# Rotation, normalisation and key splits placed on other engines in a two-layer attention kernel, with new orders for every queue

## The chip, the cores and the metric

The kernel runs on one core of a Trainium2 chip. The metric is the device time of one execution in microseconds (us). The engines are TensorE (PE; PEld is its weight load), VectorE (DVE), ScalarE (ACT), GpSimd (POOL) and SyncE (SP), whose queue issues all transfers (DMA). Each engine works through its own queue in the order in which the program wrote it; semaphores tie the queues together.

## The reference

Two layers, each an attention block and a mixture-of-adapters block, on 2048 rows of 512 (8 sequences of 256, float32). The layers differ in the attention's weights only and, in the source, in how these are stored. Cut to what matters:

```python
def attention(x, w_qkv, w_o):                 # 32 query heads, 8 key/value heads of 16
    q, k, v = split(x @ w_qkv)
    q, k = rope(q), rope(k)                   # pairs (x1, x2) -> (x1 c - x2 s, x1 s + x2 c)
    p = softmax(where(causal, q @ k.T / 4, -inf))
    return (p @ v) @ w_o

def ffn(x):                                   # 8 experts, top 2, rank 16
    w, sel = top_k(x @ gate_w.T, 2); w = softmax(w)
    return x @ base_w.T + base_b + 2 * sum(w[e] * (x @ A[e].T) @ B[e].T)

for layer in (a, b):
    x = x + attention(layernorm(x), *weights[layer])
    x = x + ffn(layernorm(x))
```

## The kernel before

**Tiles.** A tile s is one sequence of 256 rows in one layer: 16 tiles, 0 to 7 layer a, 8 to 15 layer b. The weights lie in SBUF; those of the attention are replaced between tiles 7 and 8 (`wd` fetches them into `Wst`, `wh` rounds them, `split` takes the low half). Every float32 product is done as three products of rounded and remainder parts (high and low: XH/XL, WQh/WQl, R/Rh, OH/OL).

**One tile.** `stats` (VectorE) gives mean and variance, `power` (GpSimd) the reciprocal root rs, `norm` (VectorE, L1064) the normalised rows xn, twice per norm, c = "a" ahead of attention and "f" ahead of the ffn. `tr` transposes xn on TensorE, `high` (ScalarE) and `low` (VectorE) split it. `q01` and `q2` make queries, keys and values in a PSUM tile each; `qe` (ScalarE) copies them out, the queries into R, keys and values into KV. `sw` (DMA) fetches the rows swapped in pairs into Qs. The rotation is `rc` (times cosine), `rs_` (Qs times sine), `ra` (sum), each in three parts b: 0 and 1 are halves of the queries, 2 the keys. Then `rh`, `kh` (ScalarE) round and `rl`, `kl` take the remainders, and twelve stores `st(p, 0..2)` by DMA bring R, Rh and the keys into the layout QK of four pairs of head groups p = 4 s to 4 s + 3. For each p: `A` (scores for the maxima), `Am` (VectorE, L1077, three maxima into nm), `M2` (transposes nm), `mc`, `mr` (the maxima back into QK), `B` (scores with the maximum taken off), `ex` (ScalarE, L929, exponent into PT), `causal` (GpSimd, L1237, mask, for i = 0 and 2). Two p make a half h = 2 s, 2 s + 1: `PV` (L534), `oe`, then the sums go round: `lc` (DMA), `rp` (VectorE, reciprocal), `rd`, `rr` (DMA, through memory, into NR), `mu` (GpSimd, L238, product), `oh`, `ol`. `oM` is the output product and `ox` (L1110) the residual add from PSUM. The ffn is `fA`, `fE`, `fG` (top 2), `gate_exp`, `gr`, `gt`, `fH`, `fW`, `lora_high`, `lora_low`, `fB`, `fC`, and `fx` (L1150) the second residual add; `store` and `xl` move the rows of X.

**PSUM.** There are four tiles PP0 to PP3 of [128, 2, 512]. The last arguments of a TensorE step are the tile and the release that it waits for: `q2(6, 0, 0, 3, ("qe01", 7))` goes into PP3 once `qe` has emptied the queries of tile 6.

**Order.** Each engine's queue is a list written out at the end of its block: tile s + 1's norm, products and rotation are threaded between tile s's attention and ffn. A step whose wait isn't met holds all that stands behind it on its engine. `qe(s, 0)` waits for all twelve stores of tile s - 1, since it writes R, from which they read; these in turn wait until B of four p before has read QK.

In the start, SyncE's queue is a list of loads; `kr` and `qk` lay constant rows into QK (qk waits for kr's data), and tile 0's swaps `sw(0, 0)`, `sw(0, 2)` come behind them.

## Time and profile before

| | us |
|---|---|
| median of 3 runs | 820.34 |
| range of the runs | 818.52 to 826.51 |
| the profiled execution | 823.84 |
| its span, first to last instruction | 821.8 |
| TensorE busy in the span | 685.9 (83%) |
| VectorE | 557.8 (68%) |
| GpSimd | 473.8 (58%) |
| ScalarE | 372.7 (45%) |
| mean granted TensorE clock | 0.901 of 2.4 GHz |

The profiled execution is one execution, 0.4% above the median. Busy times leave out waits and the issue of transfers. The chain of waits follows the work that ended last back from the last instruction, at each step to what released it.

### The profile page before, as it was taken

The numbers are of one execution on the slowest core, as the hardware profiler recorded it, in microseconds if no ns is written. First come the engines' busy times: TensorE is split into PE (matmuls) and PEld (weight loads), VectorE is DVE, ScalarE is ACT, GpSimd is POOL, SyncE is SP. The second block draws the span as 40 slices with busy tenths as digits, with TensorE's granted clock in tenths as the row PEclk, the third lists the DMA queues.
The fourth block names the chain that finished last, engine by engine and source line by source line (L and its number), as shares of the span: only waits on it lengthen the run. The fifth ranks groups of instructions, "written<-read, shape, count | busy, mean of one in ns | idle before, by whom it ended". The sixth has DMA issues, their size and how long they took to land.

```text
span 821.8 us, 18302 instructions
## 1 busy us (share of the span) xinstructions
PE 685.9 (83%) x7498; PEld 513.9 (63%) x7498; DVE 557.8 (68%) x786; ACT 372.7 (45%) x554; POOL 473.8 (58%) x446
## 2 busy tenths in 40 slices
PE   5826788898988897897988899887988889888996
PEld 4715565775666666665667676665667766564574
DVE  4377484766768795876868697775869686467453
ACT  2324554644544453454536464543535453453521
POOL 1124384757657593755849385865858474673621
PEclk7955959898999999798999999998999998997899
DMA  9551726163453636255452625354452725444111
GB/s 335 111 150 48 158 65 139 60 145 115 95 152 73 161 88 166 83 126 162 92 161 63 167 86 137 127 101 139 91 163 54 175 68 114 110 96 109 41 52 52
DMA packets 49650, 95.14 MB, mean 116 GB/s; under 512 B 7936, under 2 KB 19840, under 8 KB 49568
## 3 DMA queue, kind: packets, MB, share of 16 engines
q1 hardware_dynamic: 49568, 93.98, 43.6%
q8 instruction: 59, 0.97, 0.5%
q14 instruction: 23, 0.19, 0.1%
HBM read 24.42 MB, written 10.49 MB: 42 GB/s over the span
## 4 chain that ended last, share of the span: by engine, by line
PE 44%; DVE 16%; issue 13%; DMA 8%; POOL 7%; ACT 6%; SPq 5%; DVEq 0%; POOLq 0%; ACTq 0%
PE PP L428 27%; PE PP L534 11%; DVE nm L1077 5%; ACT PT L929 4%; PE PP L520 3%; POOL PT L1237 3%; DVE R L231 3%; PE PP L441 2%; POOL NE L238 2%; DMA Qs<-R 2%; DVE XL L1038 1%; DVE tw L1134 1%; DVE xn L1064 1%; DMA QK<-Rh 1%; DMA QK<-R 1%
## 5 line engine op out<-in xcount | busy, mean ns | idle before, releaser
L1077 DVE TENSOR_REDUCE nm<-PP 128x4 f32<-128x1024 f32 (+1 forms) x192 | 228.6, 1215 | 74.8 <-PE PP L428 74.2
L1237 POOL TENSOR_SCALAR_AFFINE_SELECT PT<-PT 128x1024 f32<-128x1024 f32 x128 | 144.4, 1133 | 153.8 <-ACT PT L929 153.7
L929 ACT ACTIVATE PT<-PP 128x1024 f32<-128x1024 f32 x192 | 193.2, 1026 | 83.8 <-PE PP L520 83.0
L428 PE MATMUL PP<-QK 64*128 64x128 f32 (+1 forms) x1024 | 102.6, 310 | 39.7 <-DVE nm L1077 10.5
L534 PE MATMUL PP<-PT,V 128*32 128x512 f32 x768 | 110.8, 720 | 21.0 <-POOL PT L1237 19.2
L428 PEld LDWEIGHTS PP<-QK 64*128 64x128 f32 x1024 | 85.9, 212 | 55.0 <-issue 21.6
L428 PE MATMUL PP<-XH,WQh 64*128 64x256 f32 x768 | 95.7, 299 | 6.1 <-DVE XL L1038 5.0
L520 PE MATMUL PP<-QK 64*128 64x512 f32 x384 | 83.3, 444 | 9.4 <-ACT PT L929 3.0
L428 PE MATMUL PP<-XL,WQh 64*128 64x256 f32 x768 | 91.0, 287 | 0.0
L428 PE MATMUL PP<-XH,WQl 64*128 64x256 f32 x768 | 90.8, 286 | 0.0
L238 POOL TENSOR_TENSOR NE<-NE,NR 128x512 f32<-128x512 f32 x30 | 41.2, 1374 | 69.1 <-DMA NR<-sums 69.1
L1064 DVE TENSOR_SCALAR xn<-X,mv,rs 128x512 f32<-128x512 f32 x64 | 49.3, 776 | 45.8 <-POOL rs L1228 26.7
L428 PEld LDWEIGHTS PP<-XH,WQh 64*128 64x128 f32 x768 | 69.9, 194 | 11.6 <-issue 5.2
L534 PEld LDWEIGHTS PP<-PT,V 128*32 128x32 f32 x768 | 25.5, 126 | 81.8 <-issue 60.4
L861 ACT ACTIVATE NE<-PP 128x1024 f32<-128x1024 f32 x32 | 32.8, 1024 | 86.0 <-PE PP L534 86.0
L205 POOL TENSOR_TENSOR Qs<-Qs,trig 128x512 f32<-128x512 f32 (+1 forms) x47 | 52.8, 1135 | 31.8 <-DMA Qs<-R 25.7
L428 PEld LDWEIGHTS PP<-XL,WQh 64*128 64x128 f32 x768 | 67.4, 194 | 0.6
L428 PEld LDWEIGHTS PP<-XH,WQl 64*128 64x128 f32 x768 | 67.3, 194 | 0.0
L428 PE MATMUL PP<-WOh,OH 64*128 64x512 f32 x256 | 56.1, 430 | 1.7 <-ACT mT L861 0.8
L428 PE MATMUL PP<-WBh,XH 64*128 64x512 f32 x256 | 54.5, 416 | 2.5 <-DVE glo L1114 2.3
L428 PE MATMUL PP<-WOh,OL 64*128 64x512 f32 x256 | 53.5, 408 | 0.0
L428 PE MATMUL PP<-WOl,OH 64*128 64x512 f32 x256 | 53.5, 408 | 0.0
...
## 6 DMA issues: line engine op xcount, KB each, us to landing
QK<-Rh SPq DMA_DIRECT2D x64, 256.0 KB, 4.4
...
Qs<-R SPq DMA_DIRECT2D x32, 256.0 KB, 2.4
...
```

What stands on the lines that cost most here:

```text
L205: e.tensor_tensor(schunk(b), schunk(b), trigs(1, b), ALU.mult).then_inc(S[f"rs{b}"], 1)
L231: ins = e.tensor_tensor(key_blocks(KL, q), key_tile(q), key_blocks(KH, q).bitcast(F32), ALU.subtract)
L238: e.tensor_tensor(n, n, NR[:, :], ALU.mult).then_inc(S["mu"], 1)
L428: ins = e.matmul(t[:, k, c], lhs(rows, which[k]), rhs(rows, which[k]), start=start, stop=stop, skip_group_check=True)
L441: ins = e.transpose(t[:, k, c:c + 64], source[rows, :], iden[rows, 64 * k:64 * k + 64])
L520: ins = e.matmul(PP[t][:, a, :].rearrange("p (j q) -> p j q", j=4), keys(g, a, 4 if i == 2 else 0), x[:, :, min(i, 1), :], start=True, sto ...
L534: ins = e.matmul(PP[t][32 * c:32 * c + 32, min(i, 1), :], V[:, s % 2, i // 2, 4 * G + c, :], PT[:, (3 * p + i) % RING, 512 * a:512 * a + 5 ...
L861: return e.activation(dst, src, ACT.Copy)
L929: e.activation(PT[:, k % RING, :].rearrange("p (a x) -> p a x", a=2), PP[t][:, :, :], ACT.Exp, scale=0.25).then_inc(S["ex"], 1)
L1064: e.tensor_scalar(xn[:, f, :], X[:, 2 * (s % XR) + i, :], mv[:, f, i, 0:1], rs[:, f, i:i + 1], ALU.subtract, ALU.mult).then_inc(S[c + "xn" ...
L1077: e.tensor_reduce(o, x, AX.X, ALU.max).then_inc(S["m"], 1)
L1237: e.affine_select(out=blk, in_=blk, compare_op=ALU.is_ge, fill=0.0, base=0, pattern=[[0, 8], [1, 128]], channel_multiplier=-1).then_inc(S[ ...
```

## The change

- `norm` moves from VectorE to ScalarE, as one Identity with scale rs and bias nb = -mean x rs. For it `eps` (ScalarE, two instructions of two columns) takes the place of ve's add, and `power` on GpSimd gets a second product nb.
- `rc` is no longer done in SBUF (it was on GpSimd nearly always), but on VectorE straight from PSUM, one instruction for the 1024 queries' elements and one for the keys' 256; it waits for `qe`, and for the stores of the tile before. `qe` copies into a buffer of its own, Qf, and waits only for the swaps of the tile before. The PSUM tiles are released by `rc01` and `rc2` instead of `qe01` and `qe2`.
- The rotated keys live in two blocks of KL (K2); KV is gone.
- `ra` of the keys, `rl` of both halves and `kl` are done by GpSimd (tile 0's `rs_(0, 0)`, `rs_(0, 2)`, `ra(0, 0)`, `rl(0, 0)` are VectorE's).
- The gate's difference gd is folded into the exponent (bias and scale, two instructions); te has a place of its own.
- nm has 16 columns instead of 128, and mT one buffer instead of two, so that `mc(p)` waits for `mr(p - 1)`.
- Wst is 1024 columns instead of 1536: one slot for the 768-wide weights.
- The orders of all five queues are new.

```diff
-        wland += [Wst[:, c:c + 768] for c in (0, 768, 0, 768)]
-        wland += [Wst[:, c:c + 512] for c in (0, 512, 1024, 0)]
+        wland += [Wst[:, 0:768]] * 4
+        wland += [Wst[:, c:c + 512] for c in (0, 512, 0, 512)]
 ...
+        K2 = KL.rearrange("p (n t) -> p n t", t=128)[:, 2:5:2, :]
+
+        def roped(b):
+            return QR[:, 2 * b:2 * b + 2, :].bitcast(F32) if b < 2 else K2.bitcast(F32)
 
 ...
-        def rope_rc(e, w, s, b):
-            w.wait_ge(S["c_trig"], 16)
-            w.wait_ge(S["sw01" if b < 2 else "sw2"], 32 * (s + 1))
-            e.tensor_tensor(qchunk(b), qchunk(b), trigs(0, b), ALU.mult).then_inc(S[f"rc{b}"], 1)
 ...
-            for g in range(4):
-                w.wait_ge(S[f"st{g}"], 48 * s)
 ...
             def wd(k):
-                w.wait_ge(S["wlp"], {17: 13, 18: 13, 19: 14, 20: 15, 21: 16, 22: 17, 23: 17, 24: 18}[k])
+                w.wait_ge(S["wlp"], {17: 13, 18: 14, 19: 15, 20: 16, 21: 17, 22: 17, 23: 18, 24: 19}[k])
 ...
-                x = QR.bitcast(F32) if b < 2 else KV[:, 0:1, :]
-                e.dma_start(Qs[0:P:2, c, :], x[1:P:2, :, :]).then_inc(done, 16)
-                e.dma_start(Qs[1:P:2, c, :], x[0:P:2, :, :]).then_inc(done, 16)
+                e.dma_start(Qs[0:P:2, c, :], Qf[1:P:2, c, :]).then_inc(done, 16)
+                e.dma_start(Qs[1:P:2, c, :], Qf[0:P:2, c, :]).then_inc(done, 16)
 ...
-            rows0(0); load(3); rows0(1); const("id"); load(7); load(0); rows(1); load(13); load(2); const("trig")
-            load(1); load(15); load(6); load(4); load(10); load(8); load(12); load(16); rows(3); load(5); rows(4)
-            const("iota"); rows(2); load(14); load(9); load(11); kr(); const("bias"); qk(); sw(0, 0); sw(0, 2)
 ...
+            rows0(0); rows0(1); rows(1); const("id"); load(16); load(1); load(0); const("trig"); load(6); load(5)
+            kr(); load(14); load(3); load(13); load(4); load(7); load(2); load(10); load(15); rows(3); rows(4)
+            load(8); load(9); rows(2); load(11); const("iota"); load(12); const("bias"); qk(); sw(0, 0); sw(0, 2)
+            st(0, 0); st(1, 0); st(2, 0); st(3, 0); st(0, 1); st(1, 1); st(2, 1); st(0, 2); st(3, 1); st(1, 2)
+            st(2, 2); st(3, 2); sw(1, 0); sw(1, 2); wd(17); mr(0); mr(1); st(4, 0); st(4, 1); st(4, 2); mr(2)
 ...
-            q01(6, 3, 1, 3); M2(20, 1, ("m", 62)); A(21, 0, 0, ("ex", 60)); tr("f", 6, 2, ("m", 63))
-            PV(9, 1, ("mc", 21)); tr("f", 7, 2); B(20, 0, 0, ("m", 64)); q2(6, 0, 0, 3, ("qe01", 7)); q2(6, 1, 0, 3)
 ...
+            tr("f", 6, 0, ("m", 62)); q01(6, 2, 1, 2); M2(20, 1, ("m", 63)); q01(6, 3, 1, 2); A(21, 0, 3, ("ex", 60))
+            tr("f", 7, 0); PV(9, 1, ("mc", 21)); q2(6, 0, 0, 3, ("m", 64)); q2(6, 1, 0, 3); B(20, 0, 0, ("fl", 4))
+            q2(6, 2, 0, 3); B(20, 1, 1, ("oe", 10)); q2(6, 3, 0, 3); A(21, 1, 2, ("rc01", 7)); q2(6, 0, 1, 3)
 ...
                 if b < 2:
                     w.wait_ge(S["q01"], 8 * s + 8)
-                    for g in range(4):
-                        w.wait_ge(S[f"st{g}"], 48 * s)
-                    copy(R[:, 0:1024].bitcast(F32).rearrange("p (f x) -> p f x", f=2), PP[t][:, :, :]).then_inc(
-                        S["qe01"], 1)
+                    w.wait_ge(S["sw01"], 32 * s)
+                    copy(Qf[:, 0:4, :].rearrange("p (f c) t -> p f (c t)", f=2), PP[t][:, :, :]).then_inc(S["qe01"], 1)
                 else:
                     w.wait_ge(S["q2"], 8 * s + 8)
-                    w.wait_ge(S["kl"], s)
+                    w.wait_ge(S["sw2"], 32 * s)
                     w.wait_ge(S["vt"], s)
-                    copy(KV[:, :, :], PP[t][:, :, 0:256]).then_inc(S["qe2"], 1)
+                    copy(Qf[:, 4:6, :], PP[t][:, :, 0:256]).then_inc(S["qe2"], 1)
+
+
+            def eps(c, s):
+                f = int(c == "f")
+                w.wait_ge(S["ng" + c], 2 * s + 2)
+                w.wait_ge(S["np" + c], 2 * s)
+                e.activation(ve_[:, f, :], mv[:, f, :, 1], ACT.Copy, bias=EPS).then_inc(S["ne" + c], 1)
+                e.activation(nme[:, f, :], mv[:, f, :, 0], ACT.Copy, scale=-1.0).then_inc(S["ne" + c], 1)
+
+            def norm(c, n):
+                f, i, s = int(c == "f"), n % 2, n // 2
+                w.wait_ge(S["np" + c], 2 * s + 2)
+                w.wait_ge(S[c + "t"], n)
+                e.activation(xn[:, f, :], X[:, 2 * (s % XR) + i, :], ACT.Identity, bias=nb[:, f, i:i + 1],
 ...
-                w.wait_ge(S[f"md{p % 2}"], 16 * (p // 2))
-                copy(mT[:, p % 2, :].rearrange("r (f t) -> r f t", f=2), PP[t][0:16, :, 0:64]).then_inc(S["mc"], 1)
+                if p:
+                    w.wait_ge(S[f"md{(p - 1) % 2}"], 16 * ((p + 1) // 2))
+                copy(mT[:, :].rearrange("r (f t) -> r f t", f=2), PP[t][0:16, :, 0:64]).then_inc(S["mc"], 1)
 ...
-                w.wait_ge(S["ng" + c], 2 * s + 2)
-                w.wait_ge(S["np" + c], s)
-                e.tensor_scalar(ve_[:, f, :], mv[:, f, :, 1], EPS, None, ALU.add).then_inc(S["ne" + c], 1)
-
-            def norm(c, n):
-                f, i, s = int(c == "f"), n % 2, n // 2
-                w.wait_ge(S["np" + c], s + 1)
-                w.wait_ge(S[c + "t"], n)
-                e.tensor_scalar(xn[:, f, :], X[:, 2 * (s % XR) + i, :], mv[:, f, i, 0:1], rs[:, f, i:i + 1], ALU.subtract,
-                                ALU.mult).then_inc(S[c + "xn"], 1)
 ...
+            def rc(s, b, t):
+                w.wait_ge(S["c_trig"], 16)
+                w.wait_ge(S["qe01" if b < 2 else "qe2"], s + 1)
+                for g in range(4):
+                    w.wait_ge(S[f"st{g}"], 48 * s)
+                if b < 2:
+                    e.tensor_tensor(QR.bitcast(F32), PP[t][:, :, :].rearrange("p f (c x) -> p (f c) x", c=2),
+                                    trig[:, 0, :].unsqueeze(1).to_broadcast([P, 4, 256]), ALU.mult).then_inc(S["rc01"], 1)
+                else:
+                    e.tensor_tensor(roped(2), PP[t][:, 0, 0:256].rearrange("p (q x) -> p q x", q=2), trigs(0, 2),
+                                    ALU.mult).then_inc(S["rc2"], 1)
 ...
-            stats("a", 0); norm("a", 0); split(0); norm("a", 1); split(1); low("a", 0, 0); split(2); split(3)
-            stats("a", 1); norm("a", 2); norm("a", 3); low("a", 1, 3); split(4); rs_(0, 0); split(5); rc(0, 2)
-            split(6); split(7); rc(0, 0); split(12); ra(0, 0); split(13); split(14); ra(0, 2); rl(0, 0); split(15)
-            kl(0); split(16); split(8); split(9); split(10); split(11); stats("a", 2); Am(0, 0, 0); Am(0, 1, 2)
 ...
+            stats("a", 0); split(0); split(1); low("a", 0, 0); split(2); split(3); stats("a", 1); rc(0, 0, 1)
+            rc(0, 2, 2); low("a", 1, 3); rs_(0, 0); rs_(0, 2); ra(0, 0); split(4); split(5); rl(0, 0); split(6)
+            split(7); split(12); split(13); split(14); split(15); split(16); split(8); split(9); split(10); split(11)
 ...
+            Am(20, 2, 1); Am(21, 0, 3); stats("a", 7); low("f", 3, 0); rc(6, 0, 2); Am(21, 1, 2); Am(21, 2, 0); rp(9)
 ...
-                w.wait_ge(S["ne" + c], s + 1)
+                w.wait_ge(S["ne" + c], 2 * s + 2)
                 w.wait_ge(S[c + "xn"], 2 * s)
                 e.tensor_tensor(rs[:, f, :], ve_[:, f, :], half[:, :], ALU.pow).then_inc(S["np" + c], 1)
+                w.wait_ge(S["np" + c], 2 * s + 1)
+                e.tensor_tensor(nb[:, f, :], nme[:, f, :], rs[:, f, :], ALU.mult).then_inc(S["np" + c], 1)
 ...
-            causal(19, 0); power("f", 3); mu(8); causal(19, 2); ol(8); addbias(3); power("a", 7); causal(20, 0)
 ...
-            causal(23, 0); mu(10); power("f", 4); ol(10); causal(23, 2); power("a", 8); addbias(4); causal(24, 0)
 ...
+            causal(19, 0); power("f", 3); mu(8); causal(19, 2); addbias(3); ol(8); power("a", 7); rs_(6, 0)
+            causal(20, 0); ra(6, 0); rs_(6, 1); causal(20, 2); ra(6, 1); rs_(6, 2); ra(6, 2); rl(6, 0); causal(21, 0)
+            rl(6, 1); kl(6); causal(21, 2); gt(3); mu(9); fH(3); ol(9); causal(22, 0); causal(22, 2); causal(23, 0)
+            power("f", 4); mu(10); causal(23, 2); addbias(4); ol(10); power("a", 8); rs_(7, 1); causal(24, 0)
```

## Rows read from the trace of the kernel before

**Rows 1.** Three stretches: us, then busy us of PE, PEld, DVE, ACT, POOL, PEclk, DMA, GB/s.

```profile
0.00:120.00 120.00, 74.53 (x754) 60.09 (x756) 68.82 (x89) 45.30 (x67) 46.08 (x46) 0.71 0.52 146
120.00:740.00 620.00, 541.32 (x6126) 405.93 (x6125) 444.97 (x616) 300.10 (x443) 398.51 (x368) 0.94 0.46 117
740.00:821.80 81.80, 70.01 (x622) 47.85 (x620) 43.99 (x83) 27.28 (x44) 29.16 (x32) 0.88 0.21 62
sum 821.80, PE 685.86 PEld 513.87 DVE 557.77 ACT 372.69 POOL 473.75; mean PE 228.62 PEld 171.29 DVE 185.92 ACT 124.23 POOL 157.92
```

**Rows 2.** VectorE in order of time (start us, us, what): L1150 of tiles 0 and 12.

```profile
177.50 1.16 DVE L1150 TENSOR_TENSOR X<-PP,X 128x1024 f32<-128x1024 f32 x1
...
742.42 1.22 DVE L1150 TENSOR_TENSOR X<-PP,X 128x1024 f32<-128x1024 f32 x1
```

**Rows 3.** What TensorE waited for (us in total, times, longest us).

```profile
PE PP L534 <- POOL PT L1237: 19.2, 6, 4.1
PE PP L441 <- DVE xn L1064: 19.2, 7, 5.1
...
PE PP L428 <- DVE nm L1077: 10.8, 12, 1.9
```

**Rows 4.** Chain of waits around 420 us (start us, us, what).

```profile
419.08 3.69 issue
422.81 1.26 POOL NE L238
...
424.77 1.60 DVE xn L1064
```

**Rows 5.** The five us behind one stall, columns as in rows 1.

```profile
189.00:194.00 5.00, 5.00 (x24) 0.79 (x16) 3.11 (x5) 1.03 (x1) 3.99 (x3) 0.50 0.33 104
```

**Rows 6.** Chain of waits in the start.

```profile
26.62 10.53 DMA Qs<-R
...
45.64 1.06 ACT Rh L861
```

**Rows 7.** TensorE in order of time, its first long stands (idle before, releaser).

```profile
50.97 0.48 PE L441 MATMUL PP<-iden,KV 64*128 64x64 f32 x4 [13.10 <-ACT KV L861]
...
57.33 2.08 PE L428 MATMUL PP<-QK 64*128 64x128 f32 x16 [5.88 <-issue]
```

**Rows 8.** VectorE's groups: xcount | busy us, mean ns | idle before.

```profile
L1064 DVE TENSOR_SCALAR xn<-X,mv,rs 128x512 f32<-128x512 f32 x64 | 49.3, 776 | 45.8 <-POOL rs L1228 26.7 <-PE PP L441 19.1
...
L231 DVE TENSOR_TENSOR R<-KV,R 128x384 fp32r<-128x384 f32 (+1 forms) x32 | 33.6, 1088 | 0.8 <-ACT R L861 0.7
...
L1110 DVE TENSOR_TENSOR X<-PP,X 128x1024 f32<-128x1024 f32 x16 | 19.6, 1222 | 7.8 <-PE PP L428 7.7
...
L215 DVE TENSOR_TENSOR R<-R,Rh 128x512 fp32r<-128x512 f32 x16 | 18.2, 1138 | 3.7 <-ACT Rh L861 3.7
L210 DVE TENSOR_TENSOR KV<-KV,Qs 128x256 f32<-128x256 f32 x16 | 14.0, 876 | 0.9 <-POOL Qs L205 0.9
...
L1058 DVE TENSOR_SCALAR ve<-mv 128x2 f32<-128x2 f32 x32 | 11.8, 368 | 1.1
```

**Rows 9.** The tile xn: duration ns min/median/max.

```profile
L1064 DVE TENSOR_SCALAR xn<-X,mv,rs x64: 532/546/2099, 7.6 to 802.7; 128x512 f32<-128x512 f32 x64
```

**Rows 10.** Two of ScalarE's groups.

```profile
L861 ACT ACTIVATE OH<-NE 128x512 fp32r<-128x512 f32 x32 | 20.0, 624 | 72.6 <-POOL NE L238 69.6 <-DVE NE L238 3.0
...
L861 ACT ACTIVATE R<-PP 128x1024 f32<-128x1024 f32 x16 | 16.4, 1022 | 56.7 <-DMA QK<-Rh 26.8 <-DMA QK<-R 20.7 <-PE PP L428 9.1
```

**Rows 11.** Two of GpSimd's groups.

```profile
L200 POOL TENSOR_TENSOR R<-R,trig 128x512 f32<-128x512 f32 x30 | 41.2, 1383 | 0.0
...
L1263 POOL TENSOR_TENSOR wsel<-gx,wsel 128x2 f32<-128x2 f32 x16 | 6.2, 390 | 17.1 <-DVE wsel L1130 17.1
```

**Rows 12.** SyncE's queue in the start.

```profile
24.01 0.77 SPq L364 DMA_DIRECT2D QK<-NE  x1
```

**Rows 13.** DMA issues: count, KB each, median us from issue to landing.

```profile
Qs<-R SPq DMA_DIRECT2D x32, 256.0 KB, 2.4
```

More of the change, by code:

```diff
@@ L508, in M2 @@
                 w.wait_ge(S["m"], 3 * p + 3)
-                w.wait_ge(S["mz"], 1)
                 released(free)
-                cross(PP[t], 0, nm[:, p % 2, :]).then_inc(S["mt"], 1)
+                for k, rows in enumerate((UP, LO)):
+                    ins = e.transpose(PP[t][0:16, k, 0:64], nm[rows, p % 2, :], iden[rows, 64 * k:64 * k + 64])
+                ins.then_inc(S["mt"], 1)
             def B(p, i, t, free=None):
@@ L908, in kh @@
                 w.wait_ge(S["ra2"], s + 1)
-                for g in range(4):
-                    w.wait_ge(S[f"st{g}"], 48 * s)
                 for q in range(2):
@@ new lines, in _ @@
+            ex(5, 1, 0); ex(5, 2, 1); mc(6, 3); kh(2); oe(2, 0); mc(7, 1); oh(1); ex(6, 0, 0); ex(6, 1, 1)
+            ex(6, 2, 0); ex(7, 0, 1); ex(7, 1, 0); norm("a", 8); ex(7, 2, 1); eps("f", 0); oh(2); qe(3, 0, 2)
+            norm("f", 0); oe(3, 0); norm("f", 1); mc(8, 3); high("f", 0, 1); ex(8, 0, 3); qe(3, 2, 2); ex(8, 1, 1)
+            ve(3, 1); mc(9, 0); fe(0, 3); ex(8, 2, 2); norm("a", 9); rh(3); gate_exp(0); high("a", 4, 3); kh(3)
+            ex(9, 0, 2); ex(9, 1, 0); ex(9, 2, 2); mc(10, 3); oh(3); oe(4, 2); mc(11, 0); lora_high(0, 2)
@@ new lines, in _ @@
+            ex(15, 1, 1); eps("f", 2); norm("f", 4); ex(15, 2, 1); norm("f", 5); qe(5, 0, 3); mc(16, 0)
+            high("f", 2, 2); oh(6); eps("a", 6); oe(7, 1); ex(16, 0, 2); ex(16, 1, 1); norm("a", 12); ex(16, 2, 1)
+            qe(5, 2, 0); mc(17, 2); norm("a", 13); fe(2, 3); ve(5, 2); high("a", 6, 1); rh(5); ex(17, 0, 0)
+            gate_exp(2); kh(5); ex(17, 1, 0); ex(17, 2, 3); mc(18, 1); oh(7); oe(8, 1); lora_high(2, 0); mc(19, 1)
+            ex(18, 0, 1); ex(18, 1, 0); ex(18, 2, 1); ex(19, 0, 0); ex(19, 1, 1); eps("f", 3); norm("f", 6)
@@ new lines, in _ @@
+            norm("a", 22); ex(36, 2, 3); qe(10, 2, 2); mc(37, 1); norm("a", 23); fe(7, 0); ve(10, 1)
+            high("a", 11, 3); rh(10); ex(37, 0, 2); gate_exp(7); kh(10); ex(37, 1, 2); ex(37, 2, 0); mc(38, 3)
+            oh(17); oe(18, 0); lora_high(7, 2); mc(39, 0); ex(38, 0, 0); ex(38, 1, 2); ex(38, 2, 0); ex(39, 0, 1)
+            ex(39, 1, 3); eps("f", 8); norm("f", 16); ex(39, 2, 3); norm("f", 17); qe(11, 0, 0); mc(40, 2); oh(18)
+            high("f", 8, 1); eps("a", 12); oe(19, 2); ex(40, 0, 1); ex(40, 1, 2); norm("a", 24); qe(11, 2, 3)
@@ new lines, in _ @@
+            ex(40, 2, 0); ve(11, 3); mc(41, 1); fe(8, 2); norm("a", 25); rh(11); gate_exp(8); high("a", 12, 0)
+            ex(41, 0, 1); kh(11); ex(41, 1, 2); ex(41, 2, 0); mc(42, 2); oh(19); oe(20, 2); lora_high(8, 1)
+            mc(43, 2); ex(42, 0, 2); ex(42, 1, 1); ex(42, 2, 2); ex(43, 0, 1); ex(43, 1, 0); eps("f", 9)
+            norm("f", 18); ex(43, 2, 0); norm("f", 19); qe(12, 0, 2); mc(44, 3); high("f", 9, 1); oh(20)
+            eps("a", 13); oe(21, 3); ex(44, 0, 1); ex(44, 1, 3); norm("a", 26); ex(44, 2, 3); qe(12, 2, 0); mc(45, 1)
@@ L1028, in _ @@
+            lora_high(13, 3); high("f", 14, 0); fe(14, 3); eps("f", 15); gate_exp(14); norm("f", 30); norm("f", 31)
+            lora_high(14, 1); high("f", 15, 2); fe(15, 3); gate_exp(15); lora_high(15, 2)
         @block.vector
@@ new lines, in _ @@
+            rl(3, 1); kl(3); causal(9, 0); causal(9, 2); gt(0); mu(3); fH(0); ol(3); causal(10, 0); causal(10, 2)
+            causal(11, 0); power("f", 1); mu(4); causal(11, 2); addbias(1); ol(4); power("a", 5); rs_(4, 1)
+            causal(12, 0); rs_(4, 0); causal(12, 2); ra(4, 0); ra(4, 1); rs_(4, 2); ra(4, 2); rl(4, 0); rl(4, 1)
+            kl(4); causal(13, 0); causal(13, 2); gt(1); mu(5); fH(1); ol(5); causal(14, 0); causal(14, 2)
+            causal(15, 0); power("f", 2); mu(6); causal(15, 2); addbias(2); ol(6); power("a", 6); rs_(5, 1)
@@ new lines, in _ @@
+            rs_(10, 0); ra(10, 1); ra(10, 0); causal(36, 2); rs_(10, 2); ra(10, 2); rl(10, 0); causal(37, 0)
+            rl(10, 1); kl(10); causal(37, 2); gt(7); mu(17); fH(7); ol(17); causal(38, 0); causal(38, 2)
+            causal(39, 0); power("f", 8); mu(18); causal(39, 2); addbias(8); ol(18); power("a", 12); rs_(11, 1)
+            causal(40, 0); rs_(11, 0); ra(11, 1); ra(11, 0); causal(40, 2); rs_(11, 2); rl(11, 0); ra(11, 2)
+            rl(11, 1); causal(41, 0); kl(11); causal(41, 2); gt(8); mu(19); fH(8); ol(19); causal(42, 0)
```

965 lines of the change are left out of this document (466 added, 499 removed).

## The prediction

> **What bounds the kernel now.** I read first the busy times of three stretches [rows 1]. TensorE is busy 541.3 of the 620 us between 120 and 740 us, VectorE 445.0, GpSimd 398.5, ScalarE 300.1. The layers are in a steady rhythm there: the second residual add ends tile 0 at 177.5 us and tile 12 at 742.4 us [rows 2], so a tile takes 564.9 / 12 = 47.1 us, of which TensorE works about 41. Nothing can go below that, and what can be won in the middle is 620 - 541.3 = 78.7 us of idle time, plus what the clock lost: it was granted at 0.94 of full speed there [rows 1]. The first 120 us are another matter: TensorE is busy only 74.5 us, at 0.71.
>
> Which wait ends last? TensorE's list of waits [rows 3] puts 19.2 us in 6 waits on the causal mask of GpSimd (PT), 19.2 us in 7 waits on the normalised rows of VectorE (xn), and 10.8 us in 12 waits on the maxima (nm). The chain of waits shows that the first two are one thing [rows 4]: once in a tile GpSimd stands at `mu` for 3.69 us until the reciprocal sums are back from their round trip through memory (NR), and behind it in its queue stand the mask that the next PV needs or, as in these rows, the power that gives rs, and with it xn. There is a second price: the 5 us of matmuls behind such a stall ran wholly at a clock of 0.50, that is at 1.2 GHz [rows 5]: 2.5 us lost. In the start the chain shows a swap of rows that took 10.53 us to land, and 8.4 us from its landing at 37.2 until ScalarE could start the rounded copy Rh at 45.64 [rows 6]; TensorE stood 13.10 and 5.88 us behind it [rows 7].
>
> **The change, part by part.**
>
> VectorE loses the xn instructions (49.3 us), the low halves of the keys (33.6), its share of `rl` (18.2), the key sum `ra` (14.0) and ve (11.8) [rows 8]: 126.9 us. It gains `rc`, read from PSUM: per tile one of 1024 elements at 1.22 us, the price of the residual add from PSUM [rows 8], and one of 256, between a quarter of that and a half, 0.4 us: 16 x 1.62 = 26 us. Net -101 us, 557.8 to about 457. What goes is the kind that waits: xn takes 776 ns in the mean and 546 in its median [rows 8, 9], and the key subtractions average 1088 ns for 320 elements where an add from PSUM takes 1222 for 1024 [rows 8]. So VectorE's queue also becomes regular. The Trainium skill, SBUF — State Buffer, "Who interferes with whom", says that a VectorE instruction with two SBUF inputs contends with a GpSimd instruction that reads SBUF, that one with at most one such input outside the two-port modes does not, and that the loser blocks fully; rows 8 and 9 agree. Against the change speaks ScalarE: Activation LUTs, "Rules for kernel authors": adds and multiplies belong on VectorE; by that xn should stay. By the rows the copy of 512 elements on ScalarE takes 624 ns [rows 10], 78 more than an unhindered xn and 152 less than the real mean.
>
> ScalarE gains 64 x 0.624 = 40 us of xn and 64 two-column instructions (`eps`), each at most the 0.37 us of ve [rows 8]: 24 us; 372.7 becomes about 437 in 790, hidden by its idle time. GpSimd loses `rc` of 512 elements, 41.2 us [rows 11], and 15 of half that size, about 10; it gains the other `rl` (15 x 1.38 = 21), the key sums (16 x 0.7 = 11), the key subtractions (640 elements, 16 x 1.73 = 28) and 32 times nb (0.39 by the other two-column product [rows 11], 12): +21 us net, 473.8 to 495 (63% of 790). All three stay below TensorE's share, so only the waits decide.
>
> (a) Start. `kr()` is moved from behind all loads to the eleventh place of SyncE's queue. Today `qk` waits for it and goes out at 24.01 us [rows 12], after every load is out, and the swap queued behind it lands at 37.2. Without this, and with the usual 2.4 us [rows 13], the swap lands near 30: 7 us. VectorE no longer threads splits of weights between the products: from landing to Rh 3 to 4 us instead of 8.4 saves 4 to 5. Against that the new `rc(1, 0)` stands at the head of VectorE until all twelve stores of tile 0 have landed, in front of the first maximum: 5 us back; and xn now stands behind `wh` on ScalarE. Net 7, and 2 more because tile 1's swap starts before the stores. I take -9; ends 0 (the stores still last as long) and -19 (13.10 + 5.88, all of it).
>
> (b) The mid-tile stall. `power("f", s)` stands before `mu` in nearly every tile, where `mu` stood first in half of them: the xn kind (19.2 us) goes. The mask still stands behind `mu`, and the last transposition of xn now stands ahead of PV: the PT kind will come where xn's was, but about 1 us shorter. I take half of 38.4 away: -19; ends 0 and -38.
>
> (c) The clock. Granted 0.94 means half speed for 12% of 620 us = 74 us, 37 us of delay. Half of the stalls gone, but many of those left are still long enough: a quarter, -9; ends 0 and -19.
>
> (d) The maxima. VectorE is 15% less loaded and has no blocked instruction left but `te` and the splits: half of 10.8, -5; ends 0 and -11.
>
> (e) `qe` no longer waits for the stores: 26.8 + 20.7 us of ScalarE's waits [rows 10] leave ScalarE's queue. They do not vanish: `rc` has them on VectorE, but later in the tile (behind `low("f")`), where the stores will mostly have landed. The two banks are held longer by 1.22 and 0.4 us; the next users stand behind four to six other matmul steps, which hide this. With the cover gone it is 1.6 us a tile. I take +8 in all for new waits, with the single mT; ends 0 and +49 (13 tiles x (26.8 / 12 + 1.6)).
>
> (f) Weights of layer 2. Wst is one slot of 768 columns, so each of wd(18) to wd(20) waits for the split before it, on SyncE ahead of stores. A landing of 384 KB is 1.5 x 2.4 = 3.6 us; three in a row are 11 us, mostly beside the half tile (23 us) between the last `q2` of tile 7 and the first `q01` of tile 8. +3; ends 0 and +11.
>
> (g) Tail: two more hops in the norm (eps, nb), 0.4 + 0.4 us, twice in line: +1. Narrower nm (16 columns): nothing; M2 sends the same 64 columns through.
>
> Sum: -9 - 19 - 9 - 5 + 8 + 3 + 1 = -30. The profiled execution took 823.84 us around its span of 821.8: about 794. It is 0.4% above the median of the runs, 820.34, so I predict **790 us**.
>
> **Rivals.**
> Slower: `rc` at the head of VectorE's queue still waits for the stores, and maxima, masks and then TensorE queue behind it. For it: the wait was real on ScalarE (26.8 us over some 12 tiles), VectorE feeds TensorE more directly, and both PSUM banks wait with it. Against it: the later place. Priced at the whole +49 in place of +8 it gives 794 + 41 = 835, as a median 832 us. It outweighs the gains from 38 / 13 = 2.9 us per tile on.
> No change: the bound of a tile is the round trip of the sums, which the change leaves as it is; the mask stays behind `mu`, each tile keeps one stall of 3 to 4 us and its clock loss. Then only the start, less (f) and (g), is won: 820 - 5 = 815 us. For it: GpSimd's order still has `mu` before the last mask.
> Faster still: with VectorE free, stalls and clock losses go almost wholly: (b) -38, (c) -19, (d) -8, start -9, new waits +4, (f, g) +4: -66, which is 758, or 755 as a median; half way there from the forecast, 772.
>
> **How the numbers follow.** My forecast (775 to 805) has 0.58, the slower rival 0.15, no change 0.13, faster still 0.14. The range reaches from 770, half of the last case, to 822, which takes in no change and leaves most of the slower rival out. Between two measurements of this kernel 1% is about what can be told. Faster by over 1% (below 812): 0.58 + 0.14 + a little of the third, 0.74; within 1%: 0.12; slower: 0.14.
>
> **What would show it.** (a) right: Rh of tile 0 starts near 34 us, and the first maximum near 51 (twelve stores at 1 us of issue each, 3 us to land, `rc`); wrong: later than 55. (b) right: TensorE's waits on PT and xn together near 20 us, xn's nearly none. (c) right: 0.95 or more between 100 and 700. (d): waits on nm below 6 us. (e) wrong if VectorE's waits list shows `rc` waiting for QK stores over 1 us a tile in the middle. (f) wrong if one tile about 350 us is over 52 us long. The forecast fails altogether if the tile's rhythm stays at 47 us.

## The result, and the profile after

The changed kernel takes 749.75 us (median; 748.29 to 754.0), the kernel before 819.43 us beside it: 0.918 of it, 95% interval 0.911 to 0.925. That is 70 us faster; 790 was predicted. The profiled execution has a span of 752.0 us against 821.8.

The stretches of [rows 1], with the second cut and the end 70 us earlier (us, busy us of PE, PEld, DVE, ACT, POOL, PEclk, DMA, GB/s), after:

```profile
0.00:120.00 120.00, 86.16 (x900) 66.37 (x902) 66.75 (x81) 61.63 (x96) 56.69 (x62) 0.77 0.59 160
120.00:670.00 550.00, 506.36 (x5944) 389.47 (x5942) 354.59 (x493) 335.61 (x541) 379.88 (x396) 0.96 0.50 128
670.00:752.00 82.00, 71.47 (x662) 48.23 (x658) 38.27 (x70) 34.91 (x61) 32.51 (x38) 0.94 0.24 67
sum 752.00, PE 663.98 PEld 504.07 DVE 459.61 ACT 432.15 POOL 469.07; mean PE 221.33 PEld 168.02 DVE 153.20 ACT 144.05 POOL 156.36
```

TensorE does the same work in 664.0 instead of 685.9 us (its granted clock is 0.926 instead of 0.901) and idles 88 instead of 136 us. Where in time that lies shows when the cuts are put at events of the work: the first maximum on VectorE, the second residual add of tile 0, that of tile 12, the end. The kernel before, then after:

```profile
58.49:177.50 119.01, 97.41 (x964) 73.54 (x964) 76.85 (x94) 56.76 (x79) 69.96 (x63) 0.79 0.40 99
177.50:742.42 564.92, 492.25 (x5594) 368.65 (x5592) 410.46 (x567) 272.12 (x404) 363.64 (x336) 0.94 0.46 119
742.42:821.80 79.38, 67.59 (x604) 45.89 (x600) 42.26 (x82) 27.16 (x44) 29.16 (x32) 0.88 0.19 59
```

```profile
52.17:157.34 105.17, 90.79 (x932) 65.85 (x934) 61.56 (x70) 59.98 (x91) 68.33 (x70) 0.83 0.43 97
157.34:674.03 516.69, 475.75 (x5596) 366.15 (x5592) 334.81 (x464) 317.58 (x511) 357.62 (x372) 0.96 0.50 130
674.03:752.00 77.97, 67.46 (x618) 45.09 (x618) 34.44 (x67) 33.10 (x58) 29.92 (x35) 0.94 0.20 63
```

So 6.3 us are won until the first maximum, 13.8 from there to the end of tile 0, 48.2 over the next twelve tiles (47.1 to 43.1 us each), 1.4 in the tail. Of the 48.2, 16.5 are TensorE's busy time (492.3 to 475.8) and 31.7 its idle time (72.7 to 40.9).

TensorE's waits, in the answer to [rows 3], after:

```profile
PE PP L531 <- POOL PT L1258: 19.1, 8, 3.4
PE PP L437 <- ACT xn L901: 10.0, 5, 5.0
PE PP L424 <- DMA QK<-R: 6.0, 2, 5.3
...
PE PP L507 <- DVE nm L1093: 2.9, 6, 0.7
...
PE PP L424 <- DVE nm L1093: 1.9, 4, 0.8
```

The mask's wait is there as before; xn and the maxima have shrunk. For the maxima one row of [rows 3] is not enough. Between 177.5 and 742.4 us the kernel before has four rows for nm, together 19.5 us, of which the largest two are

```profile
PE PP L428 <- DVE nm L1077: 10.0, 10, 1.9
PE PP L441 <- DVE nm L1077: 8.2, 7, 2.4
```

and the changed kernel has 4.1 us in the answering stretch: a gain of 15.4 us, somewhat more than that on PT and xn together (35.3 to 21.8).

### The profile page after: what moved, and what is told of

Its sections match the earlier page's. It is cut to its first block, busy times and chain, and to the rows that moved or that the text cites. A ratio compares the mean times of both kernels' runs of the same rounds, so it can differ in the third digit from the quotient of the medians.

```text
span 752.0 us, 18400 instructions
## 1 busy us (share of the span) xinstructions
PE 664.0 (88%) x7498; PEld 504.1 (67%) x7498; DVE 459.6 (61%) x641; ACT 432.1 (57%) x698; POOL 469.1 (62%) x494
## 4 chain that ended last, share of the span: by engine, by line
PE 59%; DMA 10%; SPq 8%; issue 7%; POOL 6%; ACT 5%; DVE 5%; POOLq 0%; DVEq 0%; ACTq 0%
PE PP L424 40%; PE PP L531 13%; PE PP L517 5%; DMA NR<-sums 3%; ACT PT L939 2%; DMA Lc<-NE 2%; SPq L285 2%; DVE nm L1093 2%; PE PP L437 2%; POOL PT L1258 2%; POOL NE L235 1%; SPq L282 1%; SPq L287 1%; SPq L314 1%; DMA Qs<-Qf 1%
## 5 line engine op out<-in xcount | busy, mean ns | idle before, releaser
L939 ACT ACTIVATE PT<-PP 128x1024 f32<-128x1024 f32 x192 | 190.8, 1022 | 62.0 <-PE PP L517 60.5
L1258 POOL TENSOR_SCALAR_AFFINE_SELECT PT<-PT 128x1024 f32<-128x1024 f32 x128 | 139.7, 1097 | 115.3 <-ACT PT L939 115.3
L531 PE MATMUL PP<-PT,V 128*32 128x512 f32 x768 | 104.1, 682 | 22.4 <-POOL PT L1258 19.1
L424 PE MATMUL PP<-QK 64*128 64x128 f32 (+1 forms) x1024 | 97.8, 298 | 19.1 <-DMA QK<-R 6.0
L424 PEld LDWEIGHTS PP<-QK 64*128 64x128 f32 x1024 | 83.5, 203 | 32.1 <-issue 14.1
L424 PE MATMUL PP<-XH,WQh 64*128 64x256 f32 x768 | 97.6, 303 | 5.2 <-DVE XL L1063 4.4
L235 POOL TENSOR_TENSOR NE<-NE,NR 128x512 f32<-128x512 f32 x30 | 38.3, 1278 | 54.0 <-DMA NR<-sums 54.0
L204 POOL TENSOR_TENSOR Qs<-Qs,trig 128x512 f32<-128x512 f32 (+1 forms) x46 | 51.1, 1116 | 27.0 <-DMA Qs<-Qf 27.0
L901 ACT ACTIVATE xn<-X,nb,rs 128x512 f32<-128x512 f32 x64 | 52.0, 812 | 19.0 <-POOL nb L1249 13.6
L517 PEld LDWEIGHTS PP<-QK 64*128 64x128 f32 x384 | 38.9, 194 | 22.5 <-issue 6.8
L209 POOL TENSOR_TENSOR R<-R,Qs 128x512 f32<-128x512 f32 (+1 forms) x47 | 52.2, 1123 | 1.3
```

The costliest lines, as they stand in the source:

```text
L204: e.tensor_tensor(schunk(b), schunk(b), trigs(1, b), ALU.mult).then_inc(S[f"rs{b}"], 1)
L209: e.tensor_tensor(roped(b), roped(b), schunk(b), ALU.add).then_inc(S[f"ra{b}"], 1)
L235: e.tensor_tensor(n, n, NR[:, :], ALU.mult).then_inc(S["mu"], 1)
L424: ins = e.matmul(t[:, k, c], lhs(rows, which[k]), rhs(rows, which[k]), start=start, stop=stop, skip_group_check=True)
L517: ins = e.matmul(PP[t][:, a, :].rearrange("p (j q) -> p j q", j=4), keys(g, a, 4 if i == 2 else 0), x[:, :, min(i, 1), :], start=True, sto ...
L531: ins = e.matmul(PP[t][32 * c:32 * c + 32, min(i, 1), :], V[:, s % 2, i // 2, 4 * G + c, :], PT[:, (3 * p + i) % RING, 512 * a:512 * a + 5 ...
```

## The experiments

Every kernel was timed beside the kernel before; its distance to the changed kernel is (its ratio - 0.9203) x 817 us, where 0.9203 is the changed kernel's own ratio in the first series (after_again) and 817 us about what the kernel before took. Each ratio is known to 0.003 to 0.009, the changed kernel's own to 0.008, so a distance to some 7 to 10 us; two rows of one series compare somewhat better. "Period" is the time from the second residual add of tile 0 to that of tile 10, by ten.

| kernel | ratio to before, 95% | distance to the changed, us | period, us |
|---|---|---|---|
| before | 1 | +65 | 46.7 |
| after_again | 0.9203 (0.912-0.928) | 0 | 42.0 |
| norm_on_vector | 0.9362 (0.928-0.945) | +13 | |
| keys_on_vector | 0.9973 (0.993-1.001) | +63 | 48.5 |
| both_on_vector | 1.0133 (1.004-1.023) | +76 | |
| keys_late | 0.9389 (0.934-0.944) | +15 | 43.5 |
| power_behind | 0.9746 (0.970-0.980) | +44 | 46.6 |
| recoupled | 0.9803 (0.974-0.987) | +49 | 45.5 |
| power_and_recoupled | 0.9899 (0.984-0.996) | +57 | 46.7 |
| power_and_keys | 0.9971 (0.994-1.000) | +63 | 48.0 |
| three_undone | 1.0107 (1.003-1.018) | +74 | 48.4 |
| late_krow | 0.9242 (0.917-0.931) | +3 | |
| dummy_two | 0.9426 (0.937-0.948) | +18 | |
| dummy_one | 0.9267 (0.921-0.932) | +5 | |
| mask_first | 0.9037, then 0.9056 (0.901-0.910) | -14, -12 | 41.1 |
| before_power_first | 1.0019 (0.998-1.006) | +67 | 47.0 |
| before_mask_first | 1.0054 (1.001-1.010) | +70 | 47.3 |
| before_early_krow | 0.9985 (0.994-1.003) | +64 | |

**The work itself, back on VectorE.** In norm_on_vector 38 of 64 xn are in VectorE's order (the expectations say 40, the trace has 38), in keys_on_vector the work on the keys, in both_on_vector both:

```diff
-ex(32, 1, 2); norm("a", 20); ex(32, 2, 2)               # ScalarE
+ex(32, 1, 2); ex(32, 2, 2)
-Am(33, 1, 0); Am(33, 2, 3)                              # VectorE
+Am(33, 1, 0); norm("a", 20); Am(33, 2, 3)
```

```diff
-rs_(9, 2); ra(9, 2); rl(9, 1); rl(9, 0); kl(9)          # GpSimd
+rs_(9, 2); rl(9, 0)                                     # GpSimd
-rc(9, 2, 1); Am(34, 0, 1); fE(6, 0); low("a", 10, 2); fG(6); Am(34, 1, 0)       # VectorE
+rc(9, 2, 1); Am(34, 0, 1); ra(9, 2); rl(9, 1); fE(6, 0); low("a", 10, 2); fG(6); kl(9); Am(34, 1, 0)
```

after_again: 

> The changed kernel as it is, for the comparison of the edits on the same chip. Both theories: 0.915 to 0.925 of the kernel before, about 750 us.

norm_on_vector: 

> The changed kernel with 40 of the 64 xn instructions (tiles 1 to 10 of the second norm, half a tile each, and tiles 5 to 13 of the first) back on VectorE as a multiply-add of one SBUF tensor with two per-partition scalars, and off ScalarE; power and nb stay on GpSimd. Theory 'release': 40 x 0.78 = 31 us more on VectorE, 8 to 12 us slower than the changed kernel. Theory 'orders': within 4 us. A third view, that ScalarE's 812 ns for xn cost time, has it 3 to 6 us faster.

keys_on_vector: 

> The changed kernel with the key sum ra(s, 2), the low half rl(s, 1) and the key subtractions kl(s) of tiles 4 to 13 back on VectorE, 40 instructions, all of them with two operands in SBUF, at the places in its order where GpSimd had them; all else, also the orders, as changed. Theory 'release' (the middle won 48 us because this kind of work no longer stands in VectorE's queue): VectorE gains 10 x 4.3 us = 43 us of busy time, about a third of the release is undone, so 12 to 18 us slower than the changed kernel, and TensorE's waits on nm rise from 9 us to over 15. Theory 'orders' (the new orders of the engines won it, whoever does the work): within 4 us of the changed kernel.

both_on_vector: 

> Both edits together: key sum, low half and key subtractions of tiles 4 to 13 and 40 of the 64 xn instructions back on VectorE, with the orders of the changed kernel. Theory 'release': 74 us more on VectorE, 25 to 35 us slower than the changed kernel, about 780 us, TensorE's waits on nm above 20 us. Theory 'orders': within 8 us of the changed kernel.

after_again came as expected, and norm_on_vector near the first theory: xn is better on ScalarE, although it takes 812 ns there. both_on_vector, at 76 us far beyond its theories, is the sum of the other two (13 + 63). keys_on_vector too was far beyond both theories, and its lists say why. VectorE's waits (us in total, times, longest), and TensorE's behind them:

```profile
DVE R L209 <- POOL Qs L204: 18.2, 10, 3.5
DVE R L228 <- ACT R L859: 16.9, 10, 3.8
```

```profile
PE PP L424 <- DVE glo L1140: 16.9, 7, 3.6
PE PP L517 <- DVE nm L1093: 10.9, 8, 3.5
```

In the places that GpSimd's order gave it, the work makes VectorE stand at the head of its queue for 35 us, until GpSimd's product (for `ra`) and ScalarE's rounded keys (for `kl`) are there; fE and the maxima queue behind. So I took the same 40 instructions to the later places of the kernel before, where what they need is there, with its order of the stores:

```diff
-rc(9, 2, 1); Am(34, 0, 1); ra(9, 2); rl(9, 1); fE(6, 0); low("a", 10, 2); fG(6); kl(9); Am(34, 1, 0)
+rc(9, 2, 1); Am(34, 0, 1); fE(6, 0); low("a", 10, 2); ra(9, 2); fG(6); Am(34, 1, 0); kl(9)
+... Am(35, 1, 1); rl(9, 1); Am(35, 2, 0)
```

> The changed kernel with the same 40 instructions back on VectorE as in keys_on_vector (key sum, low half, key subtractions of tiles 4 to 13), but at the later places where the kernel before had them, and with SyncE's stores of these tiles in the order of the kernel before, so that nothing at VectorE's head waits for GpSimd or ScalarE. Theory A (what costs is VectorE's standing at the head of its queue, 35 us in keys_on_vector, not the 43 us of work): VectorE's waits before these instructions fall under 5 us and the kernel is less than 10 us slower than the changed one. Theory B (the work itself, with the time for which it stands blocked beside GpSimd, costs): 20 to 45 us slower, with TensorE waiting for nm and glo.

VectorE's stand before `kl` is 3.7 us now instead of 16.9, before `ra` 0.5 instead of 18.2, and the kernel is 15 us slower than the changed one instead of 63. Both theories were one-sided: some 48 of the 63 us were the place in the queue (with it SyncE's order of these stores, which went back together with it), some 15 the work and its blocking.

**Is it the kind of instruction?** 44 instructions more on VectorE, with two SBUF operands or with one:

```diff
+e.tensor_tensor(Wst[:, 512:1024], bias[:, :], bias[:, :], ALU.add)          # dummy_two
+e.tensor_scalar(Wst[:, 512:1024], bias[:, :], 2.0, None, ALU.mult)          # dummy_one
```

> The changed kernel with 44 additional instructions on VectorE behind the maxima of heads 37 to 58 (5.5 tiles of layer 2): each adds a constant tile of 512 columns in SBUF to itself, two operands in SBUF, and writes it to a place that nobody reads. Theory A (a VectorE instruction with two operands in SBUF stands blocked beside a reading GpSimd): mean over 0.95 us where an undisturbed 128x512 of this kind takes 0.68, GpSimd's 128x512 products grow from 1.26 to over 1.30 us, and the time rises by 8 to 20 us. Theory B (only the load counts): mean near 0.7 us, time up by 3 to 8 us.

> The changed kernel with 44 additional instructions on VectorE at the same places as in dummy_two, but each multiplies the constant tile of 512 columns by a number: one operand in SBUF. Theory A (only the kind with two operands in SBUF is blocked): mean 0.53 to 0.60 us, time up by 1 to 6 us, less than half of what dummy_two costs. Theory B (any VectorE instruction on SBUF beside GpSimd is blocked, or only the load counts): the same rise as dummy_two within 4 us.

Their groups (xcount | busy us, mean ns) and, in the second fence of each, the durations (ns min/median/max), dummy_two first:

```profile
L1100 DVE TENSOR_TENSOR Wst<-bias 128x512 f32<-128x512 f32 x44 | 44.5, 1012 | 0.0
```

```profile
L1100 DVE TENSOR_TENSOR Wst<-bias x44: 674/784/2730, 423.0 to 663.6; 128x512 f32<-128x512 f32 x44
```

```profile
L1100 DVE TENSOR_SCALAR Wst<-bias 128x512 f32<-128x512 f32 x44 | 34.5, 783 | 0.0
```

```profile
L1100 DVE TENSOR_SCALAR Wst<-bias x44: 409/593/2593, 426.3 to 660.6; 128x512 f32<-128x512 f32 x44
```

Both kinds are held up, the first by 338 ns in the mean over its minimum, the second by 374. So dummy_one was no clean control, and its expected mean of 0.53 to 0.60 us was wrong. By the ratios it cost 5 us and the other kind 18; the two intervals do not meet, so two operands cost more, though the single profiled executions lie closer (spans 762.4 and 765.5 against 751.6). It is not the standing that differs: both kinds stand about as long, and the 10 us more of VectorE's time (44.5 against 34.5) come from the longer minimum. GpSimd pays too: its 128x512 low half (`rl`) took 1306 ns in the mean in the changed kernel, 1319 in dummy_one and 1352 in dummy_two.

**GpSimd's order around `mu`, and ScalarE's wait for the stores.** Two single undoings:

```diff
-causal(35, 0); power("f", 7); mu(16); causal(35, 2)     # GpSimd, ten tiles
+causal(35, 0); mu(16); power("f", 7); causal(35, 2)
```

```diff
 w.wait_ge(S["sw01"], 32 * s)                            # ScalarE, qe; the same for qe2
+for g in range(4):
+    w.wait_ge(S[f"st{g}"], 48 * s)
```

power_behind: 

> The changed kernel with power(f, s) moved behind mu(2s+2) on GpSimd in ten tiles, as the kernel before had it in seven. Theory A (the prediction's step b: the power behind mu is what delays xn): waits of TensorE on xn come up by 1.5 to 3 us a tile and the kernel is 12 to 25 us slower than the changed one. Theory B (the gain did not come from this order): within 4 us.

recoupled: 

> The changed kernel with ScalarE's qe made to wait again for the twelve stores of the tile before, as in the kernel before; nothing else. Theory A (the own buffer Qf takes 26.8 + 20.7 us of waits out of ScalarE's queue, and this is part of what was won in the middle): ScalarE's waits on QK come back at 20 to 45 us, and the kernel is 8 to 20 us slower than the changed one. Theory B (the stores have landed by then with the new orders): waits under 5 us, time within 3 us.

Both cost more than the upper end of what I gave them. The chain of waits of power_behind around 350 us (start us, us, what) shows the whole round trip of the sums, which now ends in xn:

```profile
339.96 1.04 ACT NE L859
341.02 3.44 DMA Lc<-NE
344.49 0.96 DVE Lc L1122
...
351.83 4.74 DMA NR<-sums
...
356.64 1.26 POOL NE L235
357.91 0.67 POOL rs L1247
...
358.88 0.82 ACT xn L901
```

It is 19 us from the copy of PV to the start of xn, and TensorE waits 3.2 to 6.1 us for that xn in each of the ten tiles: 54.9 us in 14 waits on its list. In recoupled the waits of ScalarE (first line) come back, and TensorE's two rows behind it:

```profile
ACT Qf L859 <- DMA QK<-R: 68.8, 14, 11.2
```

```profile
PE PP L531 <- ACT mT L859: 32.6, 7, 6.3
PE PP L437 <- ACT Qf L859: 22.8, 3, 12.2
```

While `qe` stands at ScalarE's head for the stores, the copy `mc` of the next heads' maxima stands behind it, and PV waits for the PSUM tile that `mc` empties. Of the 22.8 us on Qf, 12.2 are one wait before tile 0 is done.

**Do they add?**

power_and_recoupled: 

> The changed kernel with two undoings at once: power(f, s) behind mu(2s+2) in ten tiles (alone 44 us slower than the changed kernel) and qe waiting for the twelve stores again (alone 50 us). Theory A (the prediction's way of adding parts): 44 + 50 = 94 us slower than the changed kernel, about 844 us. Theory B (the two delays lie beside each other in the same stretch of a tile, so the longer one sets it): 50 to 65 us slower, 800 to 815 us.

power_and_keys: 

> The changed kernel with power(f, s) behind mu(2s+2) in ten tiles (alone 44 us slower) and the 40 instructions on the keys back on VectorE at their late places (alone about 18 us slower); qe still has its own buffer. If the parts add: 62 us slower, about 812 us. If the longer delay covers the other: 44 to 50 us slower, 795 to 801 us.

three_undone: 

> The changed kernel with three undoings at once: power behind mu, the keys late on VectorE, and qe waiting for the twelve stores. If the parts add: 44 + 18 + 50 = 112 us slower, over 860 us. If they cover each other: no slower than the kernel before, 810 to 830 us.

Power and recoupled: 44 + 49 = 93 as a sum, 57 measured. TensorE's list has 56.2 us on xn and 20.7 on Qf; the 32.6 us on mT are gone, since TensorE stands at xn in that time. Power and keys: 44 + 15 = 59 as a sum, 63 measured, so these two add within the noise. All three: 108 as a sum, 74 measured, and that is the kernel before and 9 us more. The wait for the stores lies under the other two: beside them it costs 57 - 44 = 13 and 74 - 63 = 11 us, alone 49.

**The same from the side of the kernel before.** One part alone, added to it:

```diff
-causal(31, 0); mu(14); power("f", 6); ol(14)            # before_power_first, seven tiles
+causal(31, 0); power("f", 6); mu(14); ol(14)
-power("f", 5); mu(12); causal(27, 2); ol(12)            # before_mask_first, in five tiles besides
+power("f", 5); causal(27, 2); mu(12); ol(12)
```

before_power_first: 

> The kernel before with one edit: in the seven tiles where GpSimd's order has mu(2s+2) ahead of power(f, s), power stands first. Theory A (the gains of the parts add up, as the prediction's sum has it): TensorE's 19.2 us of waits on xn nearly go and the kernel is 12 to 22 us faster than before. Theory B (several chains bound a tile in turn, and the next one takes over): less than 6 us faster, with waits on PT, R and nm in their place.

before_mask_first: 

> The kernel before with GpSimd's order alone changed: power first in seven tiles, and in five tiles (1, 3, 5, 7, 8, where ScalarE's order allows it) mu(2s+2) behind the second mask, which gave the changed kernel 12 us in ten tiles. Theory A (parts add): the waits on PT fall by half of 25 us and it is 6 to 15 us faster than before. Theory B (in the kernel before the other chains stand beside it): within 4 us of before, with waits on exponentials, nm and R where PT was.

The first took 1.0019 (0.998 to 1.006) of the kernel before, the second 1.0054 (1.001 to 1.010). Nothing is won, while the changed kernel loses 44 us or wins 12 by the same places in ten tiles. TensorE's waits of the first:

```profile
PE PP L534 <- POOL PT L1237: 25.4, 10, 6.5
PE PP L441 <- ACT PT L929: 15.9, 6, 3.9
```

The xn of [rows 3] has left the top of the list; PT has grown from 19.2, and the exponentials (PT from ScalarE), that had 3.6 us in one wait on this line between 177 and 742 us, are at 15.9. In before_mask_first it is

```profile
PE PP L534 <- ACT mT L861: 19.9, 5, 5.8
PE PP L441 <- ACT PT L929: 15.6, 6, 4.1
```

PT of GpSimd has fallen to 6.2 us, and mT on ScalarE has its place. What holds mT and the exponentials is not `qe` but `oh`, the rounding of GpSimd's product. ScalarE's queue, first in before_power_first, then in before_mask_first (start us, us, in brackets the idle time before and its releaser):

```profile
322.59 0.63 ACT L861 ACTIVATE OH<-NE 128x512 fp32r<-128x512 f32 x1 [6.28 <-POOL NE L238]
323.13 1.00 ACT L929 ACTIVATE PT<-PP 128x1024 f32<-128x1024 f32 x1
```

```profile
377.71 0.63 ACT L861 ACTIVATE OH<-NE 128x512 fp32r<-128x512 f32 x1 [6.79 <-POOL NE L238]
378.25 0.25 ACT L861 ACTIVATE mT<-PP 16x128 fp32r<-16x128 f32 x1
```

TensorE stood 3.87 us for the first of these and 5.75 us for the second. In before_mask_first all ten stalls of over 2 us on mT or an exponential between 180 and 620 us come right behind an `oh` that had stood 3.8 to 6.8 us for `mu`. So it is still the round trip of the sums. In the kernel before it reaches TensorE over three places: `power` and the mask behind `mu` on GpSimd, and the last exponential or `mc` behind `oh` on ScalarE. The changed order moved the third one too:

```diff
-ex(23, 1, 2); oh(10); ex(23, 2, 2); mc(24, 0); qe(7, 0, 1)                   # ScalarE, kernel before
+ex(23, 2, 1); norm("f", 9); qe(7, 0, 2); mc(24, 3); high("f", 4, 0); oh(10)  # changed kernel
```

No run moves `oh` alone, in either kernel, so what that part is worth stays open. The rows fit it as the reason why the two edits above won nothing; that is argued from them, not tested.

**The start.**

```diff
-load(5); kr(); load(14); ... load(12); const("bias"); qk()         # late_krow, SyncE of the changed kernel
+load(5); load(14); ... load(12); kr(); const("bias"); qk()
```

late_krow: 

> The changed kernel with kr() moved back behind all the loads on SyncE, all else as changed. Theory A (the prediction's step a): qk waits for the landing of kr, the swap of tile 0 lands 5 to 7 us later, the first maximum comes at 57 to 60 us instead of 52.2, and the kernel is 4 to 8 us slower. Theory B (the start was won by ScalarE and VectorE, the swap is hidden): first maximum within 2 us of 52.2 and the time within 2 us.

before_early_krow: 

> The kernel before with kr() moved to the eleventh place of SyncE's queue, all else as before. Theory A (the prediction's step a): the swap of tile 0 lands 5 to 7 us earlier, near 31 us, and the kernel is 4 to 8 us faster. Theory B (VectorE's splits and the twelve stores decide the start): Rh starts within 2 us of 45.6 and the time is within 2 us of before.

The first products with the swapped rows start at 37.28 us in late_krow (31.25 in after_again) and at 30.30 in before_early_krow (37.25 before), Rh and the first maximum in before_early_krow at

```profile
39.45 1.06 ACT L861 ACTIVATE Rh<-R 128x1024 fp32r<-128x1024 f32 x1 [6.37 <-DVE R L210]
```

and 52.84 us, 6.2 and 5.7 us earlier than before [rows 6]. So the swap's price is as said, in both directions. In the time it is hardly seen: +3 us, and 0.9985 (0.994 to 1.003), that is -1 us. The traces show the step, the times do not settle how much of it is left at the end.

**A faster version.** In ten tiles the second mask stands ahead of `mu`:

```diff
-power("f", 7); mu(16); causal(35, 2); addbias(7)
+power("f", 7); causal(35, 2); mu(16); addbias(7)
```

mask_first: 

> The changed kernel with GpSimd's order turned round in ten tiles: causal(4s+7, 2), the second mask of the half tile, stands ahead of mu(2s+2) instead of behind it. Theory A (TensorE's 18 to 19 us in 8 waits on PT are the price of the mask standing behind mu): these waits fall under 8 us and the kernel is 8 to 18 us faster than the changed one. Theory B (the stall only moves to the next thing in the queue, the low halves OL and the output product): within 4 us of the changed one.

mask_first_5: 

> The same kernel as mask_first, with more rounds, to settle its distance to the changed kernel: 0.904 of the kernel before, some 12 us under the changed kernel.

It takes 740.2 us in the second run, 0.9056 of the kernel before and 12 us under the changed kernel. The waits on GpSimd's PT are gone; the longest rows of TensorE between 150 and 660 us are

```profile
PE PP L517 <- DMA QK<-mT: 7.1, 10, 1.8
PE PP L531 <- ACT mT L859: 4.4, 7, 0.7
```

with a granted clock of 0.98 from 150 to 660 us and TensorE busy for 474.4 of these 510 us.

## Why the prediction was wrong in size

The sign was right, the sum was 40 us short, and one mechanism was wrong: the step that failed is (e), the wait for the stores, which the forecast took to move to VectorE and to cost 8 us, and which all but left the kernel (putting it back costs 49 us). Two more things were missing, the first 120 us of attention and `oh` on ScalarE; (b), (c) and (d) were mis-sized. By the rows of the traces the gain of 69.8 us of span splits so:

| part | forecast, us | by the rows, us |
|---|---|---|
| (a) to the first maximum | -9 | -6.3 |
| from there to the end of tile 0 | no term | -13.8 |
| (b) PT and xn, twelve tiles | -19 | -13.5 |
| (c) TensorE's busy time, twelve tiles | -9 | -16.5 |
| (d) maxima, twelve tiles | -5 | -15.4 |
| (e), (f) and the rest of the idle time there | +11 | -2.8 |
| (g) tail | +1 | -1.4 |

Such rows say what TensorE waited for last, not what a part is worth alone; for that there are the undoings.

(a) Start, -9. Rh was forecast near 34 us and started at 34.34, the first maximum near 51 and it came at 52.17: a gain of 6.3 us there, near the 7 of the working. What failed is the reach of the terms. Step (a) ended at the first maximum, (b) to (d) were read between 120 and 740 us, and the first 120 us of attention in between had no term. They gave 13.8 us: 6.6 of clock (busy 97.4 to 90.8) and 7.2 of idle time. The kernel before waited there 7.3 us on R and 6.0 on NE, both copies of ScalarE. Ahead of the two on R it had stood at the stores (12.3 and 5.9 us), ahead of the longer one on NE (4.2 us) for 10.2 us at `oh`.

(b) Mid-tile stall, -19. PT and xn together came to 21.8 us in the middle, "near 20", xn alone to 2.7: as the prediction's sign of being right had it. The step counted what stands behind `mu` on GpSimd and left out what stands behind `oh` on ScalarE, though [rows 10] show 69.6 us of standing there for the same product. The gain by these rows is 13.5 us. The worth of the order is another matter: in the changed kernel it carries 44 us (power_behind), in the kernel before none.

(c) Clock, -9. It measured -16.5 in the middle, at 0.96. The quarter that I took was too small: I cut the clock's loss by the stalls of (b) alone, and TensorE's other stalls grew shorter too.

(d) Maxima, -5. It measured -15.4. The step read one row, 10.8 us in 12 waits, where four rows of the list, by the line of the waiting matmul, carry the same release. "Below 6 us" held for that row (1.9) and for the middle (4.1); over the whole kernel the rows on nm make 9.0.

(e) New waits, +8. This is the step that failed. `rc` waits for stores for 11.4 us in all, of it in the twelve tiles 0.3 in the one of 1024 columns and 5.8 in that of 256: half a us a tile, against the up to 49 us in all that I carried as a rival. And I set the 47.5 us that leave ScalarE's queue [rows 10] at no gain, "they do not vanish". In the changed order they do: recoupled costs 49 us, and its stall reaches TensorE over mT and Qf: 55.4 us. In the list of the kernel before hardly any of that price shows, 7.3 us on R before tile 0 is done and 4.4 us on mT in all. That it lay under the stalls on xn and PT there fits power_and_recoupled, where it costs 13 us; in the kernel before itself no run takes the wait away. An end for a gain was missing in this term's range.

(f) Weights, +3. The tile about 350 us took 54.9 us before and 44.1 after, not over 52. No loss showed.

(g) Tail, +1: it became 1.4 us shorter.

The busy times: VectorE 459.6 (457 forecast), ScalarE 432.2 (437), GpSimd 469.1 (495). GpSimd's came out lower in part since nb took 195 ns and not 390, in part since its own work grew shorter: `mu` from 1374 to 1278 ns, the low half from 1414 to 1306, the mask from 1133 to 1097. That VectorE blocks it less is the likely cause, since dummy_two brings the low half up again. xn on ScalarE took 812 ns, not 624: the copy was the wrong row for an instruction with a scale and a bias for each partition. ScalarE's total came out near only since `eps` took 0.20 us an instruction and not 0.37: 12 us more for xn, 12 less for `eps`.

Of the rivals "faster still" was nearest: it named 755 and the kernel took 750. Part of that is luck: it takes 38 us from (b), where the rows give 13.5, and nothing from the stretch behind the first maximum. It got 0.14, because I took half or a quarter of each gain. The runs show why that is the wrong way to be careful here: each tile has a few long chains (sums to xn, sums to mask, sums to `oh` to mT or exponential, stores to `qe` to mT), and some of their stalls lie in the same few us of it: power and recoupled cost 57 us together, not 93. With one left, most of its stall is there and part of the others is covered; one removed alone gave nothing (before_power_first). The work on the keys is not one of these: it adds to power. In the changed kernel the mask behind `mu` is left, worth another 12. The rival "slower" did not come: `rc` stands in VectorE's queue where the stores have landed, as was argued. "No change" was refuted by the rhythm, 43.1 us.

The removal of work from VectorE as such is the smaller part: at fitting places the keys cost 15 us on VectorE and xn 13, of some 65.
